# Causal attention of an audio tower: scores packed by heads, operands stacked from SBUF to SBUF, sums inverted in a folded layout, and the value product kept in PSUM meanwhile

## What is computed

```
xh = einsum('bsi,hoi->bhso', x, Wl) + bl      # x is the layer norm of h
Q, K, V = xh @ Wq, xh @ Wk, xh @ Wv
scores = einsum('bhsd,bhtd->bhst', Q, K)
scores = where(causal, -inf, scores)
A = softmax(scores, axis=-1)
F = einsum('bhst,bhtd->bhsd', A, V)
h = h + concat(F) @ Wo.T + bo
```

## Time and profile before

| | |
|---|---|
| median of 3 runs | 4063.19 us (4061.08 to 4069.48) |
| the profiled execution | 4064.07 us |
| its span, first to last instruction | 4062.3 us |
| mean granted TensorE clock | 0.883 |
| busy share of the span | PE 85%, DVE 49%, ACT 38%, POOL 11% |
| causal attention, of the span | about 2944 to 3622 us |
| attention, turns 1 to 14 | 3057 to 3585 us |

### The profile page before, as it was taken

The page is one execution under the profiler, slowest core; times in us unless marked ns, Lnnn a source line. Parts: engine busy times, 40 slices in busy tenths (PEclk is TensorE's granted clock), DMA queues, the critical chain, the costliest instruction groups (busy, mean ns, idle before and its releaser), DMA issues. The chain is left out here.

```text
span 4062.3 us, 51063 instructions
## 1 busy us (share of the span) xinstructions
PE 3463.0 (85%) x15954; PEld 2145.8 (53%) x15954; DVE 1972.3 (49%) x3990; ACT 1551.9 (38%) x3190; POOL 444.0 (11%) x498
## 2 busy tenths in 40 slices
PE   6499999967999899776886999999748988887998
PEld 3244444434777697433443555555435555545775
DVE  3456665643999812442243334333336666643223
ACT  2255555532444311223321444444314444432443
POOL 0000000000000000000000333333103332320000
PEclk8599999976999999887766999999859989986998
DMA  2344444421111100000002221121034434401110
GB/s 82 112 136 134 135 134 139 134 65 47 42 49 54 40 9 0 2 0 31 11 0 74 87 119 68 68 89 47 21 109 127 128 117 127 125 1 45 62 62 18
DMA packets 158169, 289.51 MB, mean 71 GB/s; under 512 B 39510, under 2 KB 113752, under 8 KB 151221
## 3 DMA queue, kind: packets, MB, share of 16 engines
q1 hardware_dynamic: 150678, 278.48, 20.7%
q10 hardware_dynamic: 7360, 9.44, 0.7%
HBM read 193.03 MB, written 94.34 MB: 71 GB/s over the span
## 5 line engine op out<-in xcount | busy, mean ns | idle before, releaser
L1171 PE MATMUL moe_o_ps<-moe_hid,moe_w 128*128 128x373 f32 x1152 | 389.9, 481 | 14.2 <-DVE moe_hid L1239 14.2
L2080 ACT ACTIVATE lstm_gate<-lstm_g_ps,lstm_w 128x373 f32<-128x373 f32 x480 | 264.5, 573 | 352.3 <-DVE lstm_state L2114 182.7
L2038 PE MATMUL lstm_g_ps<-lstm_xm,lstm_w 128*128 128x373 f32 x960 | 371.7, 484 | 8.4 <-POOL lstm_xm L1999 8.4
L398 PE MATMUL moe_h_ps<-stage_z_part,moe_wh 128*128 128x374 f32 x1152 | 339.3, 376 | 5.5 <-ACT stage_y L1186 1.7
L2556 ACT ACTIVATE caus_probsT<-caus_s_ps 128x234 f32<-128x234 f32 (+5 forms) x512 | 216.2, 438 | 299.8 <-PE caus_s_ps L2448 176.2
L2616 DVE TENSOR_REDUCE caus_nmx<-caus_a_ps 128x1 f32<-128x320 f32 (+6 forms) x512 | 235.7, 500 | 154.7 <-PE caus_a_ps L2430 133.7
L2042 PE MATMUL lstm_g_ps<-lstm_state,lstm_w 128*128 128x373 f32 x768 | 303.5, 477 | 0.0
L1171 PEld LDWEIGHTS moe_o_ps<-moe_hid,moe_w 128*128 128x128 f32 x1152 | 217.3, 191 | 127.8 <-issue 20.5
L894 DVE TENSOR_REDUCE rel_nmax<-rel_s_ps 128x1 f32<-128x746 f32 x192 | 179.2, 933 | 198.5 <-PE rel_s_ps L751 154.1
L858 ACT ACTIVATE rel_probs<-rel_s_ps,rel_nmax 128x746 f32<-128x746 f32 x192 | 170.0, 885 | 255.7 <-DVE rel_nmax L894 151.5
L1197 ACT ACTIVATE moe_ex<-moe_h_ps,moe_w 128x373 f32<-128x373 f32 x320 | 173.4, 575 | 222.8 <-PE moe_h_ps L398 221.4
(11 more groups left out here) (370 smaller groups left out, 6183.1 us busy)
## 6 DMA issues: line engine op xcount, KB each, us to landing
lstm_row<-gates SPq DMA_DIRECT2D x32, 1536.0 KB, 13.6
moe_gate<-gates SPq DMA_DIRECT2D x18, 1536.0 KB, 7.0
caus_stack<-caus_xh SPq DMA_DIRECT2D x64, 373.0 KB
caus_qs<-caus_stack SPq DMA_DIRECT2D x16, 768.0 KB, 5.7
caus_ks<-caus_stack SPq DMA_DIRECT2D x16, 768.0 KB, 8.5
caus_stack<-caus_x SPq DMA_DIRECT2D x32, 373.0 KB
moe_w<-in_moe_w SPq DMA_DIRECT2D x18, 514.0 KB, 3.6
rel_shear<-rel_probs SPq DMA_DIRECT2D x32, 256.0 KB, 2.9
```

The source lines that it names most:

```text
L398: mm = nc.tensor.matmul(out, w[i], x[j], start=(start and n == 0), stop=(stop and n == len(terms) - 1))
L1171: mm = nc.tensor.matmul(o_ps[i % 2][:, 0:HALF], w[s][:, HID + j * P:HID + (j + 1) * P], hid[i % 2][:, j, :], start=(j == 0), stop=(j == HJ ...
L2038: mm = nc.tensor.matmul(bank, w[e][:, g * P:(g + 1) * P], xm[x % 4][:], start=True, stop=(s == 0))
L2080: nc.scalar.activation(gate[x % 2][g][:], g_ps[n % RING][:, 0:HALF], ACT.Tanh if g == 2 else ACT.Sigmoid, bias=w[e][:, 9 * P + g:9 * P + g ...
```

## The change

All of it is in `causal_attention`, its two tables of pieces and its inputs.

- **Pieces.** `packed` puts as many heads into one piece as 512 columns hold (4, 2 or 1). Diagonal blocks are pieces of their own, four heads at once; the mask of such a piece is one bf16 matmul of 512 columns, and the four heads' blocks of 128 columns are added to it. There are 22 pieces a turn in each table, not 32; DVE reduces and ACT exponentiates a piece in one instruction. `probsT` and `acc` are tiles [128, 4 heads, columns], and POOL has 3 instructions a turn, not 12.
- **Stacks.** No `stack_d`: 24 DMAs a turn (L2385 of the changed kernel), each [32, 746], go from `x` and `xh` in SBUF straight to `qs` and `ks` in SBUF. The stacks have three buffers, `x` and `xh` one. ACT may write the next turn's q and k only when the 24 have landed (`moved`).
- **Inverse.** ACT copies the sums to `su` (SBUF). SP moves the four distinct rows of it (one of each head, partitions 0, 32, 64, 96) into `c_in` of 128 partitions x 24 columns. DVE takes the reciprocal there (after piece 7), SP stores `c_out` to `sums_d` in DRAM and loads it back, broadcast over 32 partitions, by four DMAs into `r`.
- **Order.** Sums of n-1 come after pieces 1 and 2. Until `r` is back the product of n-1 stays in `o_ps`; DVE multiplies after piece 13; the first three tiles of `values(n)` follow pieces 15, 16 and 17, and the other three stand at the start of the next turn. Outputs follow pieces 18 and 20.
- POOL, not DVE, fills the rows of ones of `ks`, and SP waits for it.

```diff
+def packed(tile, c0, c1):
+    out = []
+    for at in range(c0, c1, BANK):
+        w = min(BANK, c1 - at)
+        together = next(n for n in (HPG, 2, 1) if n * w <= BANK)
+        out += [(tile, at, at + w, tuple(range(h, h + together))) for h in range(0, HPG, together)]
+    return out
...
-        x = [[a.sb(f"x{i}_{j}", [P, L]) for j in range(2)] for i in range(2)]
-        xh = [[a.sb(f"xh{i}_{j}", [P, L]) for j in range(2)] for i in range(2)]
+        x = [a.sb(f"x{j}", [P, L]) for j in range(2)]
+        xh = [a.sb(f"xh{j}", [P, L]) for j in range(2)]
...
-        V_LAG, SUM_AT, OUT_AT = 4, (2, 4), (10, 12)
-        value_at = {last_of[j] + V_LAG: j for j in range(T - 1) if last_of[j] + V_LAG < NI}
+        SUM_AT, INVERT_AT, F_AT, OUT_AT = (1, 2), 7, 13, (18, 20)
+        value_at = {F_AT + 2 + k: k for k in range(3)}
         late = [j for j in range(T) if j not in value_at.values()]
...
                 m = n + 2
                 if has(m):
-                    p = m % 2
-                    for side in range(2):
+                    if has(m - STACKS):
+                        sp.wait_ge(s_full, (m - STACKS + 1) * NI)
+                    for side, dst in enumerate((qs, ks)):
                         sp.wait_ge(lo_ready, m * 2 + side + 1)
                         order = (xh, xh, x) if side == 0 else (xh, x, xh)
                         for k in range(3):
-                            sp.dma_start(stack_d[p, side, :, k * D3:(k + 1) * D3, 0:L], order[k][p][side][:]).then_inc(stores[p], 16)
-                    sp.wait_ge(stores[p], (m // 2 + 1) * 96)
...
+                            for hh in range(HPG):
+                                sp.dma_start(dst[m % STACKS][k * D3:(k + 1) * D3, hh, 0:L].bitcast(F32),
+                                             order[k][side][hh * D3:(hh + 1) * D3, :]).then_inc(moved[m % 2], 16)
+                m = n - 1
+                if has(m):
+                    ring.wait_emptied(sp, ("sum", m, 1))
+                    ring.wait_emptied(sp, ("sum", m, 0))
+                    if m > 0:
+                        sp.wait_ge(inverted, m)
+                    sp.dma_start(c_in[:], su[0:P:D3, :].rearrange("h (s c) -> h s c", c=C)).then_inc(sums_out, 16)
+                    sp.wait_ge(inverted, m + 1)
+                    if m > 0:
+                        sp.wait_ge(r_in, m * HPG * 16)
+                    sp.dma_start(sums_d.rearrange("h (s c) -> (h s) c", c=C), c_out[:]).then_inc(inverse_out, 16)
+                    sp.wait_ge(inverse_out, (m + 1) * 16)
+                    if m > 0:
+                        sp.wait_ge(f_ready, 2 * m)
+                    for hh in range(HPG):
+                        sp.dma_start(r[hh * D3:(hh + 1) * D3, :], sums_d[hh, 0:L].partition_broadcast(D3)).then_inc(r_in, 16)
...
                 if diag:
-                    mm = nc.tensor.matmul(bank[0:rows, k1 - k0 - rows:k1 - k0], identb[:, 0:rows], mask[:, 0:rows],
-                                          start=False, stop=True)
+                    start_with_mask(bank, rows, 0)
+                for at, hh in enumerate(heads):
+                    mm = nc.tensor.matmul(out[:, at, :], qs[s][0:K_S, hh, t * P:q1], ks[s][0:K_S, hh, k0:k1],
+                                          start=not diag, stop=not diag or hh == HPG - 1)
...
-                if side == 0 and half == 0 and n >= 2:
-                    act.wait_ge(stores[n % 2], n // 2 * 96)
+                if side == 0 and half == 0 and n >= 1:
+                    act.wait_ge(moved[(n - 1) % 2], ((n - 1) // 2 + 1) * 6 * HPG * 16)
...
-            def normalise(n, piece):
-                c0, c1 = SPANS[piece]
-                key = ("sum", n, piece)
-                bank = wait_full(dve, key)
-                nc.vector.reciprocal(r[:, c0:c1], bank[:, 0:c1 - c0]).then_inc(ring.free(key), 1)
-                ring.wait_emptied(dve, key)
+            def invert(n):
+                dve.wait_ge(sums_out, (n + 1) * 16)
+                if n > 0:
+                    dve.wait_ge(inverse_out, n * 16)
+                nc.vector.reciprocal(c_out[:], c_in[:]).then_inc(inverted, 1)
+
+            def normalise(n):
+                dve.wait_ge(r_in, (n + 1) * HPG * 16)
                 dve.wait_ge(v_done, (n + 1) * T)
                 if n > 0:
-                    dve.wait_ge(a_full, ring.at["out", n - 1, piece] + 1)
-                nc.vector.tensor_tensor(fT[:, c0:c1], o_ps[:, c0:c1], r[:, c0:c1], ALU.mult).then_inc(f_ready, 1)
+                    dve.wait_ge(a_full, ring.at["out", n - 1, 1] + 1)
+                for c0, c1 in SPANS:
+                    nc.vector.tensor_tensor(fT[:, c0:c1], o_ps[:, c0:c1], r[:, c0:c1], ALU.mult).then_inc(f_ready, 1)
```

More of the change, by code:

```diff
@@ L2414, in turn_maxima, with start_with_mask @@
                                     K["ident"][:]).then_inc(a_full, 1)
+            def start_with_mask(bank, rows, transposed):
+                nc.tensor.matmul(heads_of(bank[0:rows, :], range(HPG), rows), identb[0:rows, 0:rows],
+                                        masks[0:rows, transposed, :].rearrange("p (h c) -> p h c", h=HPG)[:, :, 0:rows],
+                                        start=True, stop=False)
             def row_scores(n, i):
-                t, k0, k1, hh = ROWS[i]
-                p = n % 2
+                t, k0, k1, heads = ROWS[i]
+                s = n % STACKS
                 if i == 0:
-                    pe.wait_ge(loads0[p], (n // 2 + 1) * 32)
-                if t == T - 2 and hh == 0 and k0 == 0:
-                    pe.wait_ge(loads1[p], (n // 2 + 1) * 32)
+                    pe.wait_ge(moved[n % 2], (n // 2 + 1) * 6 * HPG * 16)
                 q1 = min((t + 1) * P, L)
@@ L2543, in empty_maxima, with empty_sums @@
                 nc.scalar.copy(nmT[:], bank[0:2 * HPG * T, 0:P]).then_inc(ring.free(key), 1)
+            def empty_sums(n, piece):
+                c0, c1 = SPANS[piece]
+                key = ("sum", n, piece)
+                bank = wait_full(act, key)
+                if n > 0:
+                    act.wait_ge(sums_out, n * 16)
+                nc.scalar.copy(su[:, c0:c1], bank[:, 0:c1 - c0]).then_inc(ring.free(key), 1)
             def exponent(n, i):
-                j, q0, q1, hh = COLS[i]
+                j, q0, q1, heads = COLS[i]
                 at = n * NI + i
                 act.wait_ge(s_full, at + 1)
-                if n > 0 and hh == 0 and q0 == j * P:
+                if n > 0 and q0 == j * P:
                     act.wait_ge(v_done, (n - 1) * T + j + 1)
                     if j < POOLED:
-                        act.wait_ge(acc_done, (n - 1) * ADDS + HPG * (max(j, 1) + 1))
+                        act.wait_ge(acc_done, (n - 1) * POOLED + max(j, 1) + 1)
                     else:
@@ L2555, in exponent @@
                 rows = min(P, L - j * P)
[L2556 to L2559 removed]
+                nc.scalar.activation(probsT[j][0:rows, heads[0]:heads[-1] + 1, q0 - j * P:q1 - j * P],
+                                     heads_of(s_ps[at % 3][0:rows, :], heads, q1 - q0), ACT.Exp).then_inc(exp_done, 1)
+            act.wait_ge(filled, 4)
+            for n in range(-2, TURNS3 + 1):
                 if has(n + 2):
@@ L2570, in _ @@
                     empty_v(n + 1, 1)
-                if has(n):
-                    for i in range(NI):
+                for i in range(NI):
+                    if has(n):
                         exponent(n, i)
+                    if has(n - 1) and i in SUM_AT:
+                        empty_sums(n - 1, SUM_AT.index(i))
         @block.gpsimd
         def _(pool):
+            for i in range(STACKS):
+                nc.gpsimd.memset(ks[i][K_S:K_T, :, :].bitcast(F32), 1.0).then_inc(rows_filled, 1)
+                nc.gpsimd.memset(qs[i][K_S:K_T, :, L:LP].bitcast(F32), 0.0).then_inc(rows_filled, 1)
@@ L2697, in stage7_layout @@
         "caus_bo": f["L3_attn_bo"][:, None],
-        "causal_mask": np.where(late, -1e30, 0.0).astype(np.float32),
+        "causal_masks": np.stack([np.tile(np.where(m, -1e30, 0.0), (1, HPG)) for m in (late, late.T)], 1).astype(np.float32),
     }
```

178 lines of the change are left out of this document (79 added, 99 removed).

## The result

| | before | after |
|---|---|---|
| median of 6 runs each, side by side | 4066.76 us (4061.08 to 4072.15) | 4093.47 us (4087.62 to 4108.65) |
| the profiled execution | 4064.07 us | 4097.87 us |
| mean granted clock | 0.883 | 0.877 |

A forecast was written before the change was run, and what follows sets the result against it. TensorE was taken to bound the turn: 33.3 us of work, partly at half clock, plus about 4.4 idle. 4064.07 - 32 (turns) - 30 (start and end) = 4002, less 0.9 for the median: 4001 us, range 3960 to 4048.

The forecast's parts named there:

- The turn: Turns 1 to 14: 35.4 us each, 2.3 less than before, saving 32 us over 14 turns.
- The end: Last turns: nothing hides the inverse's chain, 8.8 us replace 5.0 of reciprocal; with the clock, +8 us.
- The start: Before turn 1: earlier moves and row scores let turn 1 begin 38 us earlier.
- the nearest issue that uses all engines takes 0.34, 0.37 with the gap, 8.9 us: SP's 24 moves in each turn: 0.37 us apiece, 8.9 us together, leaving SP free at 14.3.
- the rival "slower": SP's issue costs 0.62 us, 24 take 14.9, reciprocal holds PE at piece 10: 41.4 a turn, 4086 us; chance 0.09.
- the half clock: PE behind its gap before the values: 2.8 us of work at half clock, 1.4 to 1.5 us more a turn.
- the first premise: SP is free to issue the fold 14.3 us into a turn, after the sums are copied (about 13.5).
- The chain from the fold's issue to `r` on DVE: Inverse in each turn: fold 2.5, reciprocal 0.4, store 2.0, issues 1.1, landing 2.3, hand-overs 0.5; 8.8 us, `r` at 23.1.
- Pieces: PE's narrow blocks: pieces 0 to 21 take 16.1 us against 15.4, so +0.7 a turn (bounds 0 and +1.4).
- a sign of being wrong: On PE: the four narrow matmuls of a diagonal piece take more than 0.6 us.
- the two other signs: SP's 24 issues take over 12 us; PE waits at piece 10 for the row ring.
- The rival of half rate: Moves between 32 partitions take 11.5 us, the fold lands 2.2 later: 37.6 a turn, 4032 us; chance 0.22.

The follow-up runs named there:

- The run with 12 moves ahead: Changed kernel with SP's order alone altered: q side's 12 moves before the inverse's chain, k side's 12 after it; 4018.98 us, ratio 0.9887.
- the best run: Changed kernel with 12 moves ahead of the fold, reciprocal behind piece 5 (for 7), multiplications behind 15 (for 13); 3946.78 us, ratio 0.9699.
- the direct inverse: Changed kernel without the chain: DVE takes the reciprocal of the sums from PSUM and multiplies at once; 4001.54 us, ratio 0.9843.

## Why the prediction was wrong

The forecast was 4001 us, 62 less than the profiled execution; that came out 33.8 more. The 96 us between them are in one term of the sum. **The turn** was to be 35.4 us and is 42.3: 14 x 6.9 = 97. **The end** was to cost 8 and cost about 6 (from turn 15's split of the maxima, at 3585.2 and 3613.1, to the end of the execution). **The start** was to give 38 us and gave 36.4, and that is luck. Row scores begin at 2980.2, where I had 2971.5, and column scores at 3000.2, where I had 2993: ACT stands 16.15 us for the first 24 moves, which take 15.2 us to issue here too (2959.28 to 2974.5), not 8.9. The first turn then takes 20.4 us where I kept 26, since its clock is 1.00 from 3000.2 on, against 0.73 before.

The step that failed is "the nearest issue that uses all engines takes 0.34, 0.37 with the gap, 8.9 us". The 24 moves take 15.7, so SP is free 21.0 us into the turn (3384.5 less 3363.46), not at 14.3. I had the row of 0.62 us and gave it a chance of 0.09, since the loads of 96 partitions came near 0.34. But these read DRAM, and the 0.34 of the earlier trace rows is a store to DRAM. The trace of before has copies from SBUF to SBUF: the maxima's rows, 1.60 us for two, 0.8 each, and twelve of 8 KB in another stage, which I had not looked for:

```profile
L496 SPq DMA_DIRECT2D stage_rel<-relproj_relp x12: 624/625/817, 89.1 to 96.8; - x12
```

Their median is 0.625 us, the price of the moves. I chose the row by the number of engines where one with the same source and destination was to be had.

What followed went as the rival "slower" had it: DVE's reciprocal holds the ring, PE stands at a row piece just behind the tenth (it is 11), turns of 42.3 against its 41.4, 4093 us against 4086. The second step that failed is the half clock. I took one stretch of 2.8 us of work from the earlier trace rows, 1.5 us a turn. The run with 12 moves ahead meets the first premise, 13.6 for 14.3, and the gap, 2.7 for 2.9, and from the value tile to the next turn's start it needs 13.95 us (3342.91 to 3356.86) where I had 9.7 of work and 1.5: the clock costs 4.2 there. Its turns are shorter than that alone would make them, since the multiplications end at 23.6, not 24.2.

The other steps held. The column scores begin 6.7 us into a turn (6.8). The chain from the fold's issue to `r` on DVE takes 7.4 us (8.8): reciprocal 2.0 us behind the fold's issue, the loads of `r` 1.5 behind the store's, DVE released 3.6 after the first load. **Pieces** cost less than I took: the best run has 29.9 us of PE a turn at full clock, while I had 30.2 for the kernel before and +0.7 for narrow blocks; the four narrow matmuls of a diagonal piece and their mask take 0.62 us at full clock from start to start (3378.12 to 3378.74), not 0.71. That is over the 0.6 that I named as a sign of being wrong; the two other signs, over 12 us of issues and a wait near piece 10, came as well, and they are the ones that count. The Trainium skill, "DMA: Bandwidth & Descriptors", section "How many engines", gives these moves 16 engines. The trace agrees that it is more than four: the engines' share is 0.63 while the moves are issued (below), ten of sixteen in the mean. What I drew from the rule, that SP is then never held up, was wrong: the issue itself holds SP.

The rival of half rate had the rate about right and the turn wrong. A window within the moves:

```profile
3370.00:3384.00 14.00, 11.68 (x105) 9.10 (x107) 5.17 (x9) 7.54 (x14) 2.70 (x2) 1.00 0.63 147
```

At a share of 0.63, 147 GB/s are 14.6 for each busy engine, against 25 in the stores of before; sixteen busy ones would give some 230, an estimate from this row. The issue feeds them 146 (2.29 MB in 15.7 us), so the queue sets the pace and the rate costs nothing here. Why an engine is slower in these copies, no run shows.

## What to carry to other kernels

Price an issue from a row with the same source and destination, not by its bytes, and multiply by the count before asking how fast the data goes: 24 DMAs of 0.65 us, gaps included, were half of the best run's turn. Source and destination alone do not fix the price either: both rows are stores from SBUF to DRAM, at 0.34 and 0.62 us. Then put on that queue first whatever someone soon waits for, and check the other end of it too, where the last transfers hold a buffer. No run here puts the moves on a second queue or makes them fewer and larger. A wait on TensorE is to be costed with the clock that may be lost around it: here a gap of 2.7 us in every turn cost 4 more, gaps of 0.6 to 0.8 us cost nothing more, and those of 1.0 to 1.7 cost nothing more in 19 cases of 24.

## What the runs showed that I had not expected

- The issue of a [32, 746] DMA from SBUF to SBUF takes 0.62 us, with 16 rows or 512 columns as well, and so does that of the fold (12 KB); from DRAM 0.47; the store of [128, 24] to DRAM 0.35; the broadcast loads of `r` 0.43 each.
- The clock's loss is stepped: turns of the changed kernel are near 41 or near 44 us, those with the direct inverse 34.4 or 37.3, with the same work in each. PE's wait at row piece 11 differs little (5.0 to 5.9 us in five of the six near 41, 5.7 to 6.5 in the seven near 44); what differs is how long the clock stays at 0.50 behind it, 10.2 us in those five (as 3300.5 to 3310.7) and 17.1 in these seven (as 3341.4 to 3358.5).
- PE's busy time per turn rose from 33.3 us to 34.5 in the changed kernel and is 29.9 in the best, which has the same matmuls as the changed one: those 4.6 us are clock, not work.
